# Attention and expert block: who makes the low halves of the first normalisation

## The reference

```python
x = x + attention(groupnorm(x))   # 12 heads of 32, 7 x 7 neighbourhood plus 16 register keys
x = x + experts(groupnorm(x))     # 4 experts, top 2, gelu, hidden size 96 each
```

## Time and profile before

| what | us |
|---|---|
| median of 3 runs | 649.06 |
| the three runs | 646.35, 649.06, 655.0 |
| span of the profiled execution, first to last instruction | 648.7 |
| TensorE, Vector, ACT and Pool busy in the span | 570.3, 447.4, 308.6, 294.5 |

### The profile page before, as it was taken

How to read it: one execution, slowest core, us unless ns; L and a number is a source line. 1 busy time by engine, 2 the same in 40 slices (tenths; PEclk the granted TensorE clock), 3 DMA queues, 4 the chain that set the end, 5 groups by cost and what they waited for, 6 DMA issues and landing times.

```text
span 648.7 us, 22391 instructions
## 1 busy us (share of the span) xinstructions
PE 570.3 (88%) x9227; PEld 399.9 (62%) x9227; DVE 447.4 (69%) x1009; ACT 308.6 (48%) x609; POOL 294.5 (45%) x433
## 2 busy tenths in 40 slices
PE   3578779999899988998999988898887889998998
PEld 2336666667665866667776776655765656665554
DVE  6885575777887777775667777876688796873333
ACT  1762455215634298512663145451588337754221
POOL 3116699155222667435993362223757232313131
PEclk8799999999999998998999999899998899999999
DMA  9769674995339952397527955179651002121213
GB/s 305 181 153 287 170 203 142 222 282 152 102 77 238 242 150 67 86 261 210 154 59 172 270 170 158 33 181 264 178 141 46 3 0 74 39 74 37 74 37 109
DMA packets 130636, 94.10 MB, mean 145 GB/s; under 512 B 67132, under 2 KB 124392, under 8 KB 130536
## 3 DMA queue, kind: packets, MB, share of 16 engines
q1 hardware_dynamic: 121032, 73.85, 43.4%
q0 software_dynamic: 9504, 18.84, 9.4%
HBM read 56.29 MB, written 35.54 MB: 142 GB/s over the span
## 4 chain that ended last, share of the span: by engine, by line
PE 63%; DVE 12%; ACT 6%; issue 6%; DMA 5%; SPq 4%; POOL 3%; POOLq 0%; ACTq 0%; DVEq 0%
PE ps L1065 44%; PE ps L1229 6%; PE ps L1180 5%; PE ps L1206 4%; SPq L267 3%; DVE ST L450 2%; ACT PT L885 2%; DVE MX L558 2%; DMA QS<-MT 2%; DMA KB<-kscr 1%; ACT XH L826 1%; DMA X<-in_x 1%; SPq L250 1%; POOL vscr L361 1%; POOL X L390 1%
## 5 line engine op out<-in xcount | busy, mean ns | idle before, releaser
L558 DVE TENSOR_REDUCE MX<-ps 128x2 f32<-128x372 f32 x216 | 108.2, 540 | 65.9 <-PE ps L1180 65.2
L1065 PE MATMUL ps<-XH,WQ 128*128 128x384 f16 x810 | 142.1, 330 | 8.6 <-DVE XH L499 7.7
L1065 PEld LDWEIGHTS ps<-XH,WQ 128*128 128x128 f16 x810 | 78.0, 99 | 63.6 <-ACT XH L826 7.6
L885 ACT ACTIVATE PT<-ps 128x448 f32<-128x448 f32 (+1 forms) x162 | 78.6, 511 | 40.1 <-PE ps L1206 39.9
L1206 PE MATMUL ps<-QS,KB 122*128 122x112 f16 (+1 forms) x864 | 65.3, 215 | 18.2 <-ACT PT L885 11.9
L430 POOL TENSOR_TENSOR KT<-QS,KT 128x384 f16<-128x384 f32 x36 | 34.3, 963 | 97.2 <-ACT KT L978 97.2
L1180 PE MATMUL ps<-KB,QS 120*32 120x186 f16 x1728 | 57.4, 250 | 17.7 <-issue 6.9
L1206 PEld LDWEIGHTS ps<-QS,KB 122*128 122x128 f16 x864 | 44.1, 100 | 39.5 <-ACT PT L885 20.7
L1065 PE MATMUL ps<-WQ,XH 128*128 128x128 f16 x972 | 62.5, 223 | 4.5 <-issue 4.2
L1065 PEld LDWEIGHTS ps<-WQ,XH 128*128 128x128 f16 x972 | 56.3, 100 | 10.3 <-issue 8.1
L1229 PE MATMUL ps<-PT,VR 128*32 128x112 f32 (+1 forms) x1296 | 61.2, 263 | 1.1 <-DMA VR<-vscr 0.6
(11 more groups left out here) (168 smaller groups left out, 1005.5 us busy)
## 6 DMA issues: line engine op xcount, KB each, us to landing
KB<-kscr SPq DMA_DIRECT2D x108, 192.0 KB, 4.6
kscr<-KT SPq DMA_DIRECT2D x72, 192.0 KB, 2.5
VR<-vscr SPq DMA_DIRECT2D x216, 56.0 KB
QS<-qscr SPq DMA_DIRECT2D x108, 96.0 KB, 5.8
out<-X SPq DMA_DIRECT2D x11, 576.0 KB, 3.3
X<-in_x SPq DMA_DIRECT2D x6, 576.0 KB, 7.3
qscr<-QT POOLq DMA_DIRECT2D x18, 192.0 KB, 3.1
qscr<-PT POOLq DMA_DIRECT2D x18, 192.0 KB, 5.0
```

The source lines that it names most:

```text
L558: V.tensor_reduce(out=MX[:, s % 2, t, 2 * pair:2 * pair + 2], in_=ps[:, S_BANK(s, i), 0:2 * RUN].rearrange("p (h n) -> p h n", h=2), op=AL ...
L885: A(PTS[n % 4][:, 0:w], ps[:, ST_BANK(n), 0:w], ACT.Exp, scale=SCORE).then_inc(s_["exd"], 1)
L1065: last = mm(bank, lhsT(a, k), rhs(b, k), start=(k == 0 and n == 0), stop=(finish and k == steps - 1 and n == 2))
```

## The change

Normalisation 0 is divided anew. `POOL_K` gives all its low halves to Pool. Vector makes all three fp32 values and no low half; ACT makes high halves alone, without its fp32 value and the wait before it. Pool does strip 0's low halves, then its register-key copies, then those of the other five strips. Counts of waits follow. The arithmetic stays the same.

```diff
-POOL_K = ((), (0, 1, 2), (0, 1, 2), ())
+POOL_K = ((0, 1, 2), (0, 1, 2), (0, 1, 2), ())
...
         def tmps(n, blk, k):
-            return 2 * (n * STRIPS + blk) + k + 1
+            if n == 0:
+                return KC * blk + k + 1
+            return GN_STEPS + 2 * ((n - 1) * STRIPS + blk) + k + 1
+
+        def last_tmp(n, blk):
+            return (n - 1) * STRIPS + blk + 1
...
             def low_half(n, blk, k):            # Pool
-                if k == 2:
-                    pool.wait_ge(s_["gn_ta"], n * STRIPS + blk + 1)
+                if n and k == 2:
+                    pool.wait_ge(s_["gn_ta"], last_tmp(n, blk))
...
             for gi in range(STAGES):            # Pool
+                if gi == 0:
+                    for k in range(KC):
+                        low_half(0, 0, k)
                 register_keys(gi)
+                if gi == 0:
+                    for a in range(1, STRIPS):
+                        for k in range(KC):
+                            low_half(0, a, k)
...
                 for a in range(STRIPS):         # Vector
                     if gi == 0:
-                        for k in range(2):
+                        for k in range(KC):
                             normalised(0, a, k)
                         if a == 0:
                             weights_low(0)
-                        for k in range(KC):
-                            low_half(0, a, k)
-                        if a == 0:
                             register_low(0)
...
                 for a in range(STRIPS):         # ACT
                     if gi == 0:
-                        for k in range(2):
+                        for k in range(KC):
                             normalised(0, a, k)
-                        if dve_lows(0, a) > 0:
-                            act.wait_ge(s_["gn_lo_v"], dve_lows(0, a))
-                        A(tmp_block(0, 2), x_block(0, a, 2), ACT.Identity, ...).then_inc(s_["gn_ta"], 1)
-                        normalised(0, a, 2)
```

More of the change, by code:

```diff
@@ L386, in add_bias @@
                 pool.wait_ge(s_["gn_hi"], (img + 1) * GN_STEPS)
-                pool.wait_ge(s_["gn_t"], tmps(img, STRIPS - 1, 1))
-                pool.wait_ge(s_["gn_ta"], STRIPS * (img + 1))
+                pool.wait_ge(s_["gn_t"], tmps(img, STRIPS - 1, 1 if img else 2))
+                if img:
+                    pool.wait_ge(s_["gn_ta"], last_tmp(img, STRIPS - 1))
                 pool.wait_ge(s_["obx"], 1)
@@ L487, in normalised @@
                         dve.wait_ge(s_["gn_lo_p"], pool_lows(n, 0))
-                    dve.wait_ge(s_["gn_lo_v"], dve_lows(n, 0))
+                    if dve_lows(n, 0) > 0:
+                        dve.wait_ge(s_["gn_lo_v"], dve_lows(n, 0))
                 V.tensor_scalar(tmp_block(n, k), x_block(n, blk, k), cols["rstd"][:, k:k + 1], cols["nb"][:, k:k + 1],
@@ L495, in low_half @@
                 if k == 2:
-                    dve.wait_ge(s_["gn_ta"], n * STRIPS + blk + 1)
+                    dve.wait_ge(s_["gn_ta"], last_tmp(n, blk))
                 else:
@@ L903, in _ @@
                     if gi == 0:
-                        for k in range(2):
+                        for k in range(KC):
                             normalised(0, a, k)
-                        if dve_lows(0, a) > 0:
-                            act.wait_ge(s_["gn_lo_v"], dve_lows(0, a))
-                        A(tmp_block(0, 2), x_block(0, a, 2), ACT.Identity, bias=cols["nb"][:, 2:3], scale=cols["rstd"][:, 2:3]).then_inc(s_["gn_ta"], 1)
-                        normalised(0, a, 2)
                         if a == 0:
@@ L1106, in keys @@
                         pe.wait_ge(s_["gn_lo_p"], pool_lows(n, a + 1))
-                    pe.wait_ge(s_["gn_lo_v"], dve_lows(n, a + 1))
+                    if dve_lows(n, a + 1) > 0:
+                        pe.wait_ge(s_["gn_lo_v"], dve_lows(n, a + 1))
                 if a in (0, 1, 4, 5):
```

## The result

The change costs 0.7%, a small loss, with a ratio of 1 outside the interval: 653.41 us in the median of 20 runs against 648.74 of the kernel before, also 20 runs; ratio 1.007, 95% interval 1.0045 to 1.0094. Ratios in this document leave out slow runs, those over 1.5% above the fastest of the same kernel: one of the changed kernel here, and 12 of 29 of the kernel before in the timed runs at the end of the experiments, so that the ratios there lean upward. The profiled execution took 653.22 us with a span of 651.4. The page shows the work moved: Pool went from 294.5 to 312.5 us, Vector from 447.4 to 444.4 and ACT from 308.6 to 304.9.

What follows compares the result with a forecast made beforehand. Vector was taken to bound the first normalisation; delays of 1.65 us (strip 0), 1.65 (register copies, strip 1) and 2.9 (four cycles) sum to 6.2 on the 648.7 us span: 654.9, forecast 655.0, range 650.0 to 658.5.

Steps and rivals of the forecast that it cites:

- Rival 2: First normalisation: Pool and Vector alternate, a waiting instruction following the running one; 3.65 us a strip, 652.9 us; chance 0.20.
- Strip 0: First strip: Pool's low halves end about 24.1 us, after Vector's values and weights; first keys 1.65 us late.
- back-to-back work: Pool and Vector exclude each other in the first normalisation; whichever has continuous work keeps the other out; cycle 4.16 us.
- Strip 1: Second strip: Pool's register copies (2.34 us) precede its low halves (2.65); late by 3.3 us in all.
- The four cycles: Strips 2 to 5: mutual waiting of Pool and Vector makes each 4.16 us, adding 2.9 us to the delay.
- so TensorE is not the limit: First normalisation: first keys at 2.93 us plus key halves end at 28.5, before Pool's 29.2, so TensorE doesn't bound.
- The window copies: Strips 2 to 5: Vector's two copies wait for Pool's third low half, then take 0.47 us per cycle.
- Rival 3: TensorE's clock drops at the stage's end, slowing 45 matmuls to about 325 ns each; 6.5 us more, 661.5; chance 0.07.
- Rival 1: First normalisation: Pool and Vector don't disturb each other and Pool is faster; 2.0 us earlier, 646.9 us; chance 0.10.
- Pass-through: After the first normalisation: a shift of the last low half at 39.65 us reaches the end one for one.

Runs made afterwards that it cites:

- a_regs: Changed kernel with Pool's six register-key copies behind strip 1's low halves instead of ahead of them; 653.22 us.
- a_late_clock: Changed kernel with Vector's key low half and window copies one strip later, plus 23 matmuls of zeros before the first keys; 650.10 us (12 runs), ratio 1.0041.
- a_nocopy: a_late_clock with Vector's window copies of strips 1 to 5 cut to one element each, so the output lacks those keys; 648.81 us.
- a_clock: Changed kernel with 23 extra matmuls of zeros on TensorE before the first keys; 648.55 us.
- second profile: Changed kernel run once more without any edit, for another profile; 655.36 us.
- b_clock: Kernel before with 18 extra matmuls of zeros ahead of the register products; 648.03 us (12 runs), ratio 1.0053.
- b_pool2: b_clock with one low half of three, k = 2, moved to Pool in the first normalisation; 646.90 us (12 runs), ratio 1.0006.
- a_late: Changed kernel with Vector's key low half and window copies one strip later in its program, no extra matmuls; 654.83 us.
- a_actval: Changed kernel with ACT keeping its fp32 value of k = 2, so that only the low halves move to Pool; 650.82 us.
- mix21: Changed kernel with the low half of k = 0 given back to Vector, Pool making the other two; 651.19 us.

## Why the prediction was right, and where its reasons were not

The time was forecast as 655.0 and came at 653.4; the delay of the last keys as 6.2 us and came at 5.56. Part of that agreement is luck. Rival 2's 652.9 us lies nearer still, but its period of 3.65 us wasn't the changed kernel's either.

**Strip 0: right.** First keys forecast at 24.3, measured 24.12. Vector's third value and weights kept Pool's first low half waiting until 0.78 us after the weights, as the prediction's reading of back-to-back work had it.

**Strip 1: right in kind, too large.** Register copies took 1.62 us, not 2.34, and the keys came at 28.30 in place of 29.3. With a_regs this term's worth is 0.5 us of the end, not 1.5.

**The four cycles: right number, wrong cause.** The step that failed is "so TensorE is not the limit". It was worked out for strip 0's keys of 2.93 us and not for later strips. These took 3.04 up to strip 3 in one profile and up to strip 1 in the other, and with them the loop through two strips, which I hadn't looked for, set 4.24 us a strip. With fast keys the mutual waiting sets 3.6 to 3.84 us, so about half of the 0.9 us over before's 3.33 is the slow keys'. That is below my 4.16: from the end of Pool's third low half to its next start I had 0.47 + 1.17 - 0.13 = 1.51 us, and a_late_clock shows 0.66, because the first copy gets in before that end and Pool starts behind the first value. Against it Pool's three low halves take 3.02 us and not 2.65. I had taken back-to-back work to keep the other side out. In the strip cycle the two took turns, as rival 2 had it (a_nocopy and the narrow stretches); in strip 0 they did not, and what decides between the two is open.

**The window copies: right.** They had no row in the trace of before; beside Pool's low halves they take 1.35 us in place of 0.58, and are worth 0.46 us a strip.

**Rival 3, the clock.** I had it fall late, at the end of the stage. In the changed kernel it came the other way: the matmuls stayed slow from the start. The fall happened in variants, in a_clock, for example, and in a_late_clock, where the granted clock of the stretch from 40 to 42 us is 0.50. The prediction had no term for keys that stay slow.

**Rival 1's sum.** 2.0 us under the span of 648.7 is 646.7, not 646.9; nothing hangs on it.

**Pass-through.** A delay of 5.56 us in the profiled execution, and 4.5 in the second profile, against 4.7 between the medians of 20: it passes on whole, within the scatter. The exponentials on ACT, which stand in all six stages, show how it travels; their summaries by line, before and after:

```profile
L885 ACT ACTIVATE PT<-ps x162: 437/536/562, 74.2 to 499.4; 128x448 f32<-128x448 f32 x108, 128x352 f32<-128x352 f32 x54
...
L896 ACT ACTIVATE PT<-ps x162: 437/536/557, 79.5 to 504.1; 128x448 f32<-128x448 f32 x108, 128x352 f32<-128x352 f32 x54
```

The first comes 5.3 us later and the last 4.7 (6.0 and 6.8 in the second profile). The two profiled spans differ by only 2.7 us because the rest, from the last of these to the end, took 149.3 us in before's profile and 147.3 in both of the changed kernel. The change is an unlikely cause of that: kernels made from the kernel before have both, 149.3 us in b_clock's first profile, 147.7 in its second and 147.3 in b_pool2's.

What stays open is why the keys stay slow. Before, TensorE worked without a gap from 21.16 to 25.6 us and was fast from 26.07 on; in the changed kernel there are gaps of 1.25 and 1.14 us around the first keys. In all seven profiles with matmuls of zeros strip 1's keys were fast, 1.62 to 1.78 us. In the six of the changed division without them they took 3.04 in three (both of the changed kernel, a_late) and 1.6 to 1.9 in three (a_actval, a_regs, mix21). So filling goes with fast keys, but they come without it too. What decides it in a given run I haven't shown.

## What to carry to other kernels

Before moving work to an idle engine, follow the new chain through the program order of every engine that it passes, over more than one turn of the loop: here Pool needed 2.65 us of a 3.33 us period and the stage still slowed down, since each of its turns now hung on TensorE's keys of two strips before, and with these fast, on turns with Vector. In these rows Pool's subtractions and Vector's copies, values and two-input operations hold each other up; count their times as a sum, turn by turn, and allow for a wait over more than one instruction. And check whether a matmul's duration, taken from the kernel before, is that of a fast or a slow stretch, since the fast pace can come later in the changed kernel, as it did in two profiles here.

## What the runs showed of the hardware

Three rows of the table of stretches, the first of the changed kernel, the others of a_clock:

```profile
36.00:40.00 4.00, 3.04 (x9) 1.19 (x9) 2.96 (x6) 2.18 (x5) 2.64 (x3) 0.50 0.38 87
...
24.00:25.00 1.00, 0.86 (x3) 0.44 (x4) 0.60 (x2) 0.99 (x2) 1.00 (x4) 1.00 0.85 350
...
42.00:43.00 1.00, 0.19 (x1) 0.00 (x0) 0.34 (x2) 0.59 (x1) 1.00 (x2) 0.50 1.25 282
```

The third number from the end is the granted clock. In the changed kernel it is 0.50 where nine keys matmuls take 3.04 us, and the trace's records of the clock have it there from 13.0 to 40.3 us; strip 4's keys, at 41.07, are fast. In the profile of before they have 0.50 from 11.7 to 25.3, and the keys are fast from 26.07. In a_clock nine keys matmuls at 24.14 us took 3.04 too, yet the column reads 1.00. That 1.00 is not a reading: the trace has no record of the clock before 27.5 us in this execution, and before 32.0 in the second profile of the changed kernel, and the column shows 1.00 where there is none. From the first record on, clock and pace agree in the rows of both. So before a profile's first record the durations of the matmuls are the only reading.

The 18 matmuls of zeros took 3.68 us from 17.49 on in a_clock and didn't bring the fast pace by 24.14.

Pool's subtraction and Vector's instructions hold each other up at prices that repeat in these rows: a value that waits for one of Pool's low halves ends 0.22 us after it, and two window copies beside Pool's low halves take 1.35 us in place of 0.58. The key low half, which Vector reads from PSUM, takes 0.61 us at 36.67 in a_late_clock, in the middle of Pool's three (35.45 to 38.47), as it does with Pool idle.
